# Attention plus routed experts on one core: ScalarE copies the attended values after the exponentials, and the transfer queue loads expert weights one slot later in its order

## What is computed

```python
x = x + xattn(layernorm(x), ctx, Wq, Wkv, Wproj, bproj)
    # softmax(q k^T / 8) v, 16 heads of 64, then @ Wproj + bproj
x = x + ffn(layernorm(x), gate_w, expert_w, expert_b, combine_w)
    # top 2 of softmax(x gate^T); w * silu(x W_e^T + b_e) summed; then @ combine^T
```

## Time and profile before

| | us |
|---|---|
| median of three runs | 2218.74 |
| lowest, highest | 2216.15, 2225.38 |
| the profiled execution | 2207.19 |
| its span, first to last instruction | 2204.3 |
| TensorE busy | 1689.9 (77%) |
| VectorE busy | 1225.8 (56%) |
| ScalarE busy | 1062.2 (48%) |
| GpSimd busy | 922.7 (42%) |

### The profile page before, as it was taken

One profiled execution on the slowest core, in us unless ns is written; L12 is line 12 of the kernel. 1 busy time (PEld: TensorE's weight loads), 2 busy tenths in 40 slices (PEclk: granted clock), 3 DMA queues, 4 the chain that ended last, 5 costly groups with the idle time before them and its releaser, 6 DMA issues.

```text
span 2204.3 us, 39447 instructions
## 1 busy us (share of the span) xinstructions
PE 1689.9 (77%) x11835; PEld 1586.3 (72%) x11835; DVE 1225.8 (56%) x3090; ACT 1062.2 (48%) x2904; POOL 922.7 (42%) x1213
## 2 busy tenths in 40 slices
PE   4578898978777778888777777988777778876565
PEld 4578888877767777877777776877777777865454
DVE  5357777766545556776554455666555556643222
ACT  4356566645444445655444444655444445633232
POOL 3335555544333334655333333554333345534032
PEclk9889999999998989999989899999999999987767
DMA  5343332334444444334444454335454453447785
GB/s 177 123 139 82 88 86 77 82 91 130 140 143 135 136 136 127 94 109 144 145 141 146 135 158 147 94 109 171 145 159 133 141 153 113 137 145 231 237 257 175
DMA packets 219978, 303.79 MB, mean 138 GB/s; under 512 B 24725, under 2 KB 184698, under 8 KB 219258
## 3 DMA queue, kind: packets, MB, share of 16 engines
q1 hardware_dynamic: 207482, 267.71, 40.5%
q0 software_dynamic: 12288, 33.57, 5.0%
HBM read 164.06 MB, written 70.01 MB: 106 GB/s over the span
## 4 chain that ended last, share of the span: by engine, by line
PE 38%; DMA 23%; SPq 14%; issue 10%; DVE 8%; POOL 4%; ACT 3%; another core or an unknown queue 0%; POOLq 0%; DVEq 0%; ACTq 0%
DMA k_s<-qk_s 21%; PE s_ps L483 10%; PE gen_ps L483 10%; PE o_ps L483 8%; PE proj_ps L483 4%; SPq L359 4%; PE qk_ps L483 3%; SPq L413 3%; SPq L414 2%; SPq L416 2%; ACT probs L717 2%; PE pT_ps L521 2%; DVE sums L881 1%; DVE pT_s_lo L832 1%; POOL o_s_lo L1134 1%
## 5 line engine op out<-in xcount | busy, mean ns | idle before, releaser
L690 ACT COPY stage<-o_ps 64x256 f32<-64x256 f32 x512 | 188.3, 368 | 801.8 <-PE o_ps L483 788.7
L483 PE MATMUL s_ps<-k_s,qk_s 128*128 128x256 f32 x1536 | 264.8, 313 | 284.2 <-DMA k_s<-qk_s 269.3
L483 PEld LDWEIGHTS s_ps<-k_s,qk_s 128*128 128x128 f32 x1536 | 221.0, 209 | 312.2 <-DMA k_s<-qk_s 297.5
L874 DVE TENSOR_REDUCE neg_max<-s_ps 128x4 f32<-128x512 f32 x256 | 176.5, 690 | 367.0 <-PE s_ps L483 365.1
L881 DVE TENSOR_REDUCE sums<-probs 128x4 f32<-128x512 f32 x256 | 175.6, 686 | 358.4 <-ACT probs L717 358.4
L1132 POOL CAST o_s_hi<-stage 128x256 fp32r<-128x256 f32 x256 | 103.6, 405 | 628.0 <-ACT stage L690 627.3
L1123 POOL TENSOR_TENSOR probs<-probs,inv_sums 128x512 f32<-128x512 f32 x256 | 266.6, 1042 | 222.6 <-DVE inv_sums L883 222.6
L717 ACT ACTIVATE probs<-s_ps,neg_max 128x128 f32<-128x128 f32 x1024 | 292.9, 369 | 29.3 <-DVE neg_max L874 22.8
L483 PE MATMUL proj_ps<-wproj_s_hi,o_s_hi 128*128 128x256 f32 x512 | 158.8, 310 | 89.3 <-POOL o_s_lo L1134 71.1
L1134 POOL TENSOR_TENSOR o_s_lo<-stage,o_s_hi 128x256 fp32r<-128x256 f32 x256 | 187.8, 734 | 21.1
L1154 POOL DMA_INDIRECT stage<-sorted_y,y_row_of x128 | 126.3, 987 | 146.9 <-issue 64.0
(11 more groups left out here) (169 smaller groups left out, 4854.7 us busy)
## 6 DMA issues: line engine op xcount, KB each, us to landing
w_block<-expert_table SPq DMA_DIRECT2D x163, 512.0 KB
k_s<-qk_s SPq DMA_DIRECT2D x512, 128.0 KB
stage<-sorted_x SPq DMA_DIRECT2D x163, 128.0 KB
sorted_y<-stage SPq DMA_DIRECT2D x163, 128.0 KB
x_raw<-in_x SPq DMA_DIRECT2D x32, 256.0 KB
c_raw<-in_ctxT SPq DMA_DIRECT2D x32, 256.0 KB
stage<-in_x SPq DMA_DIRECT2D x32, 256.0 KB
x_kept<-x SPq DMA_DIRECT2D x32, 256.0 KB
```

What stands on the lines that cost most here:

```text
L483: mm = pe.matmul(out_ap, l, r, start=start and n == 0, stop=stop and n == len(terms) - 1, skip_group_check=skip)
L690: last = act.copy(to, of)
L874: dve.tensor_reduce(neg_max[p % 2][:, :], s_ps[:, :].rearrange("p (k n) -> p k n", k=4), AX_X, ALU.max, negate=True).then_inc(max_done, 1)
```

## The change

1. On ScalarE `attended` is called right after `exps` and is, counted from there, one slot later: `attended(u-2)` behind `exps(u)`, in place of `attended(u-1)` at the end of the slot before.
2. `load_block` is cut in two. `load_rows` stays with the block turned in s+2; `load_expert` (weights and bias) is called for the block turned in s+1. `store_block` comes after both and is called for the block turned in s-3.
3. `qk_s` and `k_s` get another order of axes, so that the high and low part of one head's keys lie beside each other: a key transfer moves the same 128 KB in runs of 2 KB.

```diff
-        qk_s = [sb(f"qk_s{b}", [P, 2, 2 * N2], F32R) for b in range(2)]
+        qk_s = [sb(f"qk_s{b}", [P, 2, 2, N2], F32R) for b in range(2)]
...
-                    sp.dma_start(k_s[p % 2][rows, :, h, :].bitcast(F32),
-                                 qk_s[p % 2][rows, :, N2:].bitcast(F32)).then_inc(k_in[p % 2], 16)
+                    sp.dma_start(k_s[p % 2][rows, h, :, :].bitcast(F32),
+                                 qk_s[p % 2][rows, 1, :, :].bitcast(F32)).then_inc(k_in[p % 2], 16)
...
-            def load_block(c, b, n):
+            def load_rows(c, b, n):
                 r = n % RING
                 if b == 0:
                     sp.wait_ge(blocks_done, c + 1)
                     for half in range(2):
                         wait(sp, scattered[half], 64 * ((plan.ends[c] + 1 - half) // 2))
+                    sp.wait_ge(cleared, 16 * E * (c + 1))
+                if n == 0:
+                    sp.wait_ge(dump_cleared, 16)
+                wait(sp, made["turn_block"], n - RING + 1)
+                row = sp.value_load(blocks[b:b + 1, c, 0:1], min_val=0, max_val=ROWS - P)
+                sp.dma_start(x_block[r], sorted_x[bass.ds(row, P), :]).then_inc(x_block_in[r], 16)
+
+            def load_expert(c, b, n):
+                r = n % RING
...
                 wait(sp, made["expert"], n - RING + 1)
                 e = sp.value_load(blocks[b:b + 1, c, 1:2], min_val=0, max_val=E)
                 sp.dma_start(w_block[r][:, :, :].bitcast(F32).rearrange("p a n -> p (a n)"),
...
-                if s - 2 in plan.turn:
-                    store_block(*plan.turn[s - 2])
                 if s + 2 in plan.turn:
-                    load_block(*plan.turn[s + 2])
+                    load_rows(*plan.turn[s + 2])
+                if s + 1 in plan.turn:
+                    load_expert(*plan.turn[s + 1])
+                if s - 3 in plan.turn:
+                    store_block(*plan.turn[s - 3])
...
                 if now:
                     exps(i, u)
+                if u < 2 and before:
+                    attended(i - 1, 6 + u)
+                if u >= 2 and now:
+                    attended(i, u - 2)
...
                 if s in plan.mix:
                     weigh(plan.mix[s])
-                if u == 0 and before:
-                    attended(i - 1, 7)
-                if u > 0 and now:
-                    attended(i, u - 1)
```

More of the change, by code:

```diff
@@ L399, in load_block @@
                         wait(sp, scattered[half], 64 * ((plan.ends[c] + 1 - half) // 2))
+                    sp.wait_ge(cleared, 16 * E * (c + 1))
[6 more added lines that the diff above has]
+                r = n % RING
+                if b == 0:
+                    sp.wait_ge(blocks_done, c + 1)
                 if n < RING:
@@ L403, in load_block @@
                     sp.wait_ge(table_stored[r], 16 * count)
-                if b == 0:
-                    sp.wait_ge(cleared, 16 * E * (c + 1))
                 if n == 0:
                     sp.wait_ge(bias_stored, 96)
[L408 to L411, removed]
                 wait(sp, made["expert"], n - RING + 1)
@@ L512, in scores @@
                     mm = products(s_ps[:, t * N2:(t + 1) * N2].rearrange("p (h n) -> p h n", h=2), three(
-                        (0, 1), (0, 1), lambda part: qk_s[p % 2][:, part, t * P:(t + 1) * P],
-                        lambda part: k_s[p % 2][:, part, :, t * P:(t + 1) * P]))
+                        (0, 1), (0, 1), lambda part: qk_s[p % 2][:, 0, part, t * P:(t + 1) * P],
+                        lambda part: k_s[p % 2][:, :, part, t * P:(t + 1) * P]))
                 mm.then_inc(s_made, 1)
@@ L723, in qk @@
                 wait(act, s_made, n - 1)
-                split_hi(qk_made, n + 1, [(qk_s[p % 2][:, 0, :], qk_ps[:, :])], qk_hi)
+                split_hi(qk_made, n + 1, [(qk_s[p % 2][:, :, 0, :], qk_ps[:, :].rearrange("p (g n) -> p g n", g=2))], qk_hi)
             def pT(j, p):
@@ L886, in qk @@
                 split_lo(qk_hi, j * HEAD_PAIRS + p + 1, [
-                    (qk_s[p % 2][:, 1, :], qk_ps[:, :], qk_s[p % 2][:, 0, :])], qk_lo)
+                    (qk_s[p % 2][:, :, 1, :], qk_ps[:, :].rearrange("p (g n) -> p g n", g=2), qk_s[p % 2][:, :, 0, :])], qk_lo)
             def pT(j, p):
```

## The result

The changed kernel takes 1884.08 us (median of four runs, 1881.10 to 1887.86) against 2217.44 us of four runs of the kernel before: 0.8499 of it, 95% interval 0.8461 to 0.8536. The forecast was 1985 and the range ended at 1915, so it is faster as forecast, and by more than the range held. The profiled execution took 1882.66 us, its span is 1880.2, which is 324.1 us less than the 2204.3 before.

A forecast was written before the change was run, and what follows sets the result against it. Keys held in SyncE's queue behind the expert-product wait were taken to bound block slots. 2207.2 - 284 (block slots) + 60 (quiet slots) - 10 (tail) = 1973 us profiled, 1985 as median; forecast 1950 to 2030, 8-in-10 range 1915 to 2085.

The forecast's parts named there:

- The wait at L413: SyncE's queue in block slots: waits for the expert product with ready keys behind it, 3.5 us each in the first stretch.
- the loop of the earlier trace: Block slots: scores, attend, expert product, queue wait, weights' and keys' issue, key transfer, next scores; 8.90 us, gone after the change.
- the store's move: SyncE's queue: storing a block one slot older costs nothing of itself, since VectorE has finished it by then.
- Block slots: 113 slots with blocks beside attention: 760 us against 1043.6, so -284, from 6.45 or 6.85 us a slot.
- Hand-overs: Steps between engines: raise ScalarE's 5.88 us sequence in block slots to 6.2.
- The first ten slots: Program start: set by splitting and storing expert weights through GpSimd, untouched by the change, so 0.
- Quiet slots: 133 slots without a block: lengthened by the copy's new place, +60 us, between 0 and 80.
- The closed loop: Every slot: maximum, exponentials, copy, GpSimd's two parts, projection, scores, maximum; a floor of about 5.75 us.
- The tail: Last stretch, 229.6 us: the queue is hardly held there, so -10 us, between -25 and +5.
- The runs of 2 KB: Key transfers: packets halve, bytes stay, transfer is covered; costed at 0.
- the rule on ring order: Key transfers: engines consume one queue's descriptors in order, so 3.58 us includes the weights' 512 KB; keys' transfer would shorten.
- the rival without the +60: Quiet slots: the copy's new place costs nothing, total 1925 us; chance 16%.

The follow-up runs named there:

- queue_alone: Kernel before with only the weights' load and the store called a slot later; 1 KB runs, copy in old place: 1873.49 us, 0.8546 of before.
- expert_alone: Kernel before with only the weights' load called for the block turned in s+1, store unchanged: 1959.27 us, 0.8888 of before.
- act_alone: Kernel before with only ScalarE's copy of attended values moved behind the exponentials: 2217.33 us, 1.0107 of before.
- start_first: Changed kernel with the copy back at the slot's end and the expert weights' high part ahead of it: 1844.66 us, 0.8380 of before.
- after_root: Changed kernel with GpSimd's reciprocal root of the second normalisation one slot later, behind the attended values' split: 1825.00 us, 0.8271 of before.
- after_oldact: Changed kernel with ScalarE's copy put back at the slot's end: 1866.46 us, 0.8501 of before.
- after_again: The changed kernel itself, measured again on another group's chip: 1885.69 us, 0.8558 of before.
- after_1k_again: Changed kernel with the old order of axes (keys in 1 KB runs), measured a second time: 1888.26 us, 0.8570 of before.
- after_1k: Changed kernel with the old order of axes, so keys in runs of 1 KB: 1874.01 us, 0.8537 of before.
- root_late: Changed kernel with old copy place, weights' high part ahead of the copy, and GpSimd's reciprocal root one slot later: 1778.32 us, 0.8072 of before.

## Why the prediction was wrong in size and right in kind

**The wait at L413 and the loop of the earlier trace rows: right.** The loop is gone, the weights arrive in time, the clock has gone to 1.00, and queue_alone shows that this edit alone has the gain of the block slots. The prediction took the store's move as free and of no use; expert_alone shows that it is part of the gain. Without it 36 slots take 262.4 and not 224.5 us.

**Block slots, -284 forecast, -308.3 measured.** The mean slot was 6.45 forecast and 225.3/36 = 6.26 measured without combines, 6.85 and 510.0/77 = 6.62 with them; that is 24 us. The parts of the sum came out on both sides. The forecast gave the slots 0 to 7 of a pair 5.75, 6.2, 6.9, 7.1, 6.2, 7.0, 6.2 and 6.3 us. From one row maximum to the next, pair 12 of the changed kernel has 5.54, 6.28, 6.28, 7.11, 5.60, 7.40, 6.04 and 5.80. So slot 2 with the residual (-0.6), slot 4 (-0.6) and slot 7 with the rank (-0.5) were too dear, and slot 5 with gate and values too cheap (+0.4). (The prediction's text has five slots at 6.2 or 5.75; its sum has four, and that is right for eight.) Hand-overs, of which the sum had 0.3 a slot, explain at most a part of this; what bounds each of these slots was not followed. The last eight block slots were also read too coarsely: they took 65.5/8 = 8.19 us before, were priced with the dear ones at 6.85, and took 6.0, which is 7 of the 24 us. The copy's place costs next to nothing in these slots once the queue is free: 223.9 us with the old place, 225.3 with the new.

**"The first ten slots [...] untouched: 0" failed: -28.3.** I looked for the lines of the diff in the start and found none of the queue's, and did not follow what stands behind the copy in ScalarE's order. The rule that the prediction applied to the queue, ask what is behind a wait, was not applied to the instruction that was moved. What the runs showed in place of the 0: the copy held back the weights' high part, and through GpSimd and the table's store the keys. act_alone has this gain without the queue's edit, start_first without the copy's move.

**Quiet slots, +60 forecast, +17.3 measured.** The closed loop is real, and after_root shows it as a floor. Its length was 5.55 us and not 5.75, mainly by 0.12 in the copy and 0.12 in the hand-overs; a quiet pair came to 47.1 and not 48.4. With 47.1 - 44.1 = 3.0 us on 133/8 pairs the loss would be 50. The rest of the difference is that only the first stretch, with 70 slots, lost (+19.3), while the three later ones came out at -2.0 together. The slots one by one show where: the pairs 2 to 7, which have neither blocks nor a chunk's end beside them, take 267.8 us before and 287.0 after, all of the loss of that stretch. The pairs around the ends of chunks come out level, 100.9 and 100.9 (8 and 9), 104.1 and 103.3 (16 and 17), 102.5 and 103.6 (23 and 24), 104.7 and 102.3 (29 and 30). There some slots of 9 to 11 us get shorter by about what the floor adds to others. So do slot 7 of pair 16 with slots 0 and 1 of pair 17, before (10.2, 3.9 and 9.5 us) and after (9.3, 6.8 and 6.4), columns as in the earlier trace rows:

```profile
968.00:991.60 23.60, 2.06 (x3) 0.86 0.38 109
861.60:884.00 22.40, 2.07 (x3) 0.85 0.39 116
```

The prediction let the floor cost nothing in such slots, but priced that at 12 us where it was some 30: it took all 133 slots for quiet ones and then a sixth off, when only seven whole pairs (2 to 7 and 15) are quiet. Why the long slots get shorter was not tried; after_oldact, with the copy in its old place and the new queue, takes 10.2, 3.9 and 10.0 there, so it is the copy's place that does it.

**The tail, -10 forecast, -4.8 measured**, within its bounds; two profiles of the changed kernel differ by 4 us there. **The runs of 2 KB, 0 forecast**, under 0.5% measured. The Trainium skill ("DMA: Bandwidth & Descriptors", "Why small descriptors are slow (HBM only)") has it that SBUF to SBUF transfers don't suffer from short runs; after_again and after_1k_again agree within 0.14%. The keys' median time from issue to landing is 2.5 us in after_1k as in the changed kernel. It is 3.3 in act_alone, which differs from after_1k by the queue's edit alone and ran on the same chip, so that edit shortened it. That is in line with the rule on ring order that the prediction quotes from the Trainium skill, since the 512 KB of weights no longer go right ahead of the keys, and no less with contention; no run separates the two.

Start, quiet and block slots missed by 28, 43 and 24 us, all to the same side, and the tail by 5 to the other: 90 us in the profiled spans. The range had taken them one at a time. Its lower end was the rival without the +60, and no case in it had a gain at the start or a block slot shorter than the sum of the parts.

## What to carry to other kernels

In a queue that several streams of transfers share, list for each wait what stands behind it, and do so on every engine whose order changes, in every phase of the program, the start too. When one wait ahead of an urgent transfer is taken away, look which wait is next in front of it: an edit that costs time alone can be the last quarter of the gain beside another. Moving work behind another instruction can close a loop through all engines; add up that loop once, and where it is longer than the present slot, leave the work where it was.

## What the runs showed of the hardware beyond expectation

In some quiet pairs slot 3 took 1.2 us longer than in others with the same work: 8.35 us in the pairs 3, 5 and 7 of the changed kernel, 7.1 in 2, 4 and 6. Windows of the changed kernel in pair 7, before and in the slot's projection and scores (length, PE busy, PEld, DVE, ACT, POOL, granted clock, DMA):

```profile
393.00:395.00 2.00, 0.00 (x0) 0.00 (x0) 1.80 (x3) 1.32 (x3) 1.90 (x3) 0.95 0.18 66
395.00:398.10 3.10, 2.98 (x14) 2.98 (x15) 0.06 (x2) 0.00 (x0) 2.84 (x4) 0.50 0.48 123
```

TensorE waits for the attended values, 2.35 us by the trace and all of the first window, and its clock then falls to 0.50 (1.2 GHz) for the 14 products that follow, which are the ones on the loop: projection and scores take 2.9 us there in place of 1.7. In pair 6 a wait of the same 2.35 us left the clock at 1.00, and what decides between the two is open. The Trainium skill ("TensorE: Matmul & The Clock Gate", "HAM oscillation — how this bites in real kernels") tells of waits between bursts of products after which the next burst starts at the slow clock. Pair 7 agrees with that; pair 6 does not show it. root_late moves what the attended values waited for, and its slot 3 takes 5.4 us in every pair from 2 to 7, none of them the 1.2 us longer.
